# Attention values stored before their division, their sums read back from DRAM, and copies moved earlier in SyncE's list

## What is computed

```python
xn = layernorm(x)                                  # x: 8 batches x 1024 tokens x 256
q, k, v = xn @ Wq.T, xn @ Wk.T, xn @ Wv.T          # 16 heads of q, 8 of k and v, 16 wide
energy = q @ k.T + alibi                           # per batch and head, 1024 x 1024
attn = softmax(energy / 4)
att = (attn @ v) -> concat heads
out = x + att @ Wo.T + bo + quantised_linear(xn)   # int8 weights, one scale per token
```

## Time and profile before

| | |
|---|---|
| three timed runs | 1606.62, 1609.25, 1608.16 us, median 1608.16 |
| the profiled execution | 1606.43 us, its span 1604.5 us |
| busy in the span | PE 1507.3 (94%), DVE 1394.1 (87%), ACT 1183.8 (74%), POOL 1073.4 (67%) |
| DMA | 140.98 MB, 88 GB/s, 16 DMA engines about a third busy |
| granted TensorE clock | 0.978 of 2.4 GHz on the mean |

### The profile page before, as it was taken

The page is one execution under the profiler, slowest core; times in us unless marked ns, Lnnn a source line. Parts: engine busy times, 40 slices in busy tenths (PEclk is TensorE's granted clock), DMA queues, the critical chain, the costliest instruction groups (busy, mean ns, idle before and its releaser), DMA issues.

```text
span 1604.5 us, 42517 instructions
## 1 busy us (share of the span) xinstructions
PE 1507.3 (94%) x16284; PEld 584.2 (36%) x16284; DVE 1394.1 (87%) x1698; ACT 1183.8 (74%) x2331; POOL 1073.4 (67%) x1627
## 2 busy tenths in 40 slices
PE   5789989999899998999989999899998999899999
PEld 5323323333333333333333334333333333233333
DVE  6889989999799997999979999799987988899991
ACT  3467777777687775887757887677776777688885
POOL 6457877777688875787757787577785776433332
PEclk9899999999999999999999999999999999999999
DMA  6423233343324333333333333333333332212211
GB/s 169 130 62 84 71 99 79 89 98 84 105 72 106 96 79 98 93 93 101 84 84 95 103 90 90 89 94 97 94 86 85 95 85 69 80 44 70 70 42 61
DMA packets 197291, 140.98 MB, mean 88 GB/s; under 512 B 107040, under 2 KB 165728, under 8 KB 197088
## 3 DMA queue, kind: packets, MB, share of 16 engines
q1 hardware_dynamic: 197088, 138.27, 33.0%
HBM read 81.40 MB, written 35.63 MB: 73 GB/s over the span
## 4 chain that ended last, share of the span: by engine, by line
PE 53%; DVE 31%; issue 8%; SPq 4%; DMA 3%; POOL 0%; ACT 0%; POOLq 0%; ACTq 0%
DVE row_max L999 29%; PE ps_ring L1279 17%; PE ps_pv L1355 15%; PE ps_row L1296 11%; PE ps_ring L1395 4%; PE ps_ring L1415 3%; DMA q_again<-q 2%; PE ps_ring L1398 1%; DVE pv_turned L1039 1%; PE ps_row L1279 1%; PE ps_ring L1409 1%; SPq L497 1%; PE ps_row L1387 1%; SPq L464 0%; DMA base<-x 0%
## 5 line engine op out<-in xcount | busy, mean ns | idle before, releaser
L999 DVE TENSOR_REDUCE row_max<-ps_row 128x1 f32<-128x1024 f32 x1024 | 1199.2, 1213 | 153.8 <-PE ps_row L1298 138.5
L1171 ACT ACTIVATE probs<-ps_ring 128x512 f32<-128x512 f32 x2048 | 1083.7, 601 | 284.8 <-PE ps_ring L1279 282.3
L1279 PE MATMUL ps_ring<-q,k 122*32 122x512 bf16 x8192 | 639.2, 385 | 5.6 <-DMA q<-neg_max_t 4.7
L762 POOL TENSOR_TENSOR probs<-probs,near 128x256 f32<-128x256 f32 x512 | 374.2, 731 | 368.5 <-ACT probs L1171 362.8
L1355 PE MATMUL ps_pv<-probs,v_unit 128*32 128x512 f32 x4096 | 537.9, 601 | 0.0
L1279 PEld LDWEIGHTS ps_ring<-q,k 122*32 122x32 bf16 x8192 | 216.5, 95 | 511.7 <-ACT probs L1171 324.6
L1296 PE MATMUL ps_row<-k,q 64*128 64x512 bf16 x944 | 329.7, 390 | 68.1 <-DMA q_again<-q 43.2
L1298 PE MATMUL ps_row<-k_again,q_again 64*128 64x512 bf16 x944 | 329.6, 390 | 0.0
L1296 PEld LDWEIGHTS ps_row<-k,q 64*128 64x128 bf16 x944 | 83.9, 93 | 362.9 <-issue 197.8
L1355 PEld LDWEIGHTS ps_pv<-probs,v_unit 128*32 128x32 f32 x4096 | 125.2, 110 | 55.1 <-issue 9.1
L1298 PEld LDWEIGHTS ps_row<-k_again,q_again 64*128 64x128 bf16 x944 | 83.8, 93 | 0.0
(11 more groups left out here) (84 smaller groups left out, 1009.1 us busy)
## 6 DMA issues: line engine op xcount, KB each, us to landing
parts_dram<-parts SPq DMA_DIRECT2D x59, 288.0 KB, 3.3
q_again<-q SPq DMA_DIRECT2D x63, 256.0 KB, 3.4
token_b<-token_dram SPq DMA_DIRECT2D x53, 256.0 KB, 4.0
q<-parts_dram SPq DMA_DIRECT2D x128, 96.0 KB
k<-parts_dram SPq DMA_DIRECT2D x256, 32.0 KB
q<-parts_dram SPq DMA_DIRECT2D x128, 64.0 KB
att_dram<-att_unit SPq DMA_DIRECT2D x126, 64.0 KB
att_t<-att_dram SPq DMA_DIRECT2D x56, 128.0 KB, 2.9
```

The lines of the kernel that those rows point to most:

```text
L762: pool.tensor_tensor(here, here, near[:, u % KV_HEADS, :].rearrange("p (e n) -> p e n", e=GROUP), ALU.mult).then_inc(weighted, 1)
L999: dve.tensor_reduce(row_max[:, par, e, qb:qb + 1], ps_row[qb % 2][:, :], AX_X, ALU.max, negate=True).then_inc(row_max_found, 1)
L1171: act.activation(probs[:, c % PBUFS, e, h * HALF:(h + 1) * HALF], ring_bank(u, c, e, h), ACT.Exp, scale=SCALE).then_inc(ring_freed, 1)
L1279: mm = pe.matmul(to[at, :], weights[:, at], moving, start=start, stop=stop)
```

## The change

Values are no longer turned, divided and turned back. ScalarE copies `ps_pv` as it is (`keep_pv`, one operation of 128x512 in slot 1 of the next unit), SP stores that with one DMA, and, within the loads of the next set (after its k rows), reads the sums back as 128x16 (`load_sums`). VectorE takes their reciprocal in slot 6 (`find_rsum`), SP stores it (`store_rsum`). For each pair of tiles SP loads the raw values (`load_att_t`, two DMAs) and the reciprocals spread over the 16 rows of each head (`load_att_r`, two DMAs), and GpSimd multiplies them (`share`, one operation of 128x512) in slot 0 of the odd unit, behind `weigh_near` and `shift_turned`; TensorE's `outputs` waits for that product. The last batch is projected behind its units, before as now (`project_last`, L1387); its values are now divided by VectorE (`share_last`), all but the last unit's, which are still turned, divided and turned back.

In SP's list the copies of a late set move from the end of a unit's list to its beginning, `store_att` stands ahead of the next set, and at the start the first `place_max` stands ahead of the copies of set 2 and of `load_token`.

```diff
             def load_set(u, slot, between=None):
...
+                if between is not None:
+                    load_sums(between)
...
             def store_att(u):
-                wait(sp, att_unit_ready, u + 1)
-                for e in range(GROUP):
...
+                sp.wait_ge(pv_read, u + 1)
+                sp.dma_start(att_dram[u // KV_HEADS, u % KV_HEADS].rearrange("e h r n -> (e h r) n"),
+                             att_raw[:, u % 2, :]).then_inc(att_stored[u % 2], 16)
+            def load_sums(u):
+                sp.wait_ge(att_stored[u % 2], 16 * (u // 2 + 1))
+                wait(sp, rsum_ready, u - 1)
+                sp.dma_start(sums[:, u % 2, :],
...
+            def load_att_r(t):
+                b, at = t // BLOCKS, t % BLOCKS * P
+                wait_units(rsum_stored, (b + 1) * KV_HEADS)
...
             load_set(2, 2)
+            load_again(1, 1)
...
             store_token(PREP_AHEAD)
+            place_max(0, 0)
+            load_again(2, 2)
             load_token(PREP_AHEAD)
-            load_again(1, 1)
-            load_again(2, 2)
-            place_max(0, 0)
 
             def unit(u, f):
...
+                if u + 2 < UNITS and late_set(u + 2):
+                    load_again(u + 2, (u + 2) % SETS)
+                if f["prev"]:
+                    store_att(u - 1)
                 if f["row_set"] and not late_set(u + 3):
-                    next_set(u + 3)
-                if u % PAIR == 1:
-                    store_att(u - 1)
+                    next_set(u + 3, u - 1 if f["prev"] else None)
+                elif f["prev"]:
+                    load_sums(u - 1)
...
                     place_max(u + 1, (u + 1) % SETS)
-                if f["prev"] and u % PAIR == 0:
-                    store_att(u - 1)
-                for t in f["next_att"]:
-                    load_att_t(t, t % 2)
+                for t in f["next_att"][:1]:
+                    load_att_t(t)
+                if f["prev"] and not f["last"]:
+                    store_rsum(u - 1)
                 if f["row_set"]:
                     if late_set(u + 3):
                         next_set(u + 3)
                     else:
                         load_again(u + 3, (u + 3) % SETS)
-                if u + 2 < UNITS and late_set(u + 2):
-                    load_again(u + 2, (u + 2) % SETS)
+                for t in f["next_att"][:1]:
+                    load_att_r(t)
                 for t in finished(u):
                     store_out(t, t % 2)
...
+            def share(t):
+                pool.wait_ge(att_t_loaded, 16 * 2 * EC * (t // PAIR + 1))
+                pool.tensor_tensor(att_t[:, :, :], att_t[:, :, :], att_r[:, :, :],
+                                   ALU.mult).then_inc(att_t_ready, 1)
...
-                    if c == 3 and f["prev"] and u % PAIR == 0:
-                        norm(u - 1)
+                    if c == 0:
+                        for t in f["proj"][:1]:
+                            share(t)
...
+                        if i == 13 and f["prev"]:
+                            find_rsum(u - 1)
...
+            def keep_pv(u):
+                act.wait_ge(pv_done, BLOCKS * (u + 1))
+                wait(act, att_stored[u % 2], 16 * (u // 2))
+                act.activation(att_raw[:, u % 2, :], ps_pv[:, :], ACT.Copy).then_inc(pv_read, 1)
...
+                    if c == 1 and f["prev"]:
+                        keep_pv(u - 1)
...
-                        pe.wait_ge(att_t_loaded[t % 2], 16 * (t // 2 + 1))
+                        pe.wait_ge(att_t_ready, t // PAIR + 1)
```

More of the change, by code:

```diff
@@ L64 @@
 V_COLS = 32
+SUMS = GROUP * SEQ // P
 LN_EPS = 1e-5
@@ L450, in wait_parts, with load_set @@
                     wait(sp, parts_stored[t % 2], 16 * len(range(t, tiles, 2)))
-            def load_set(u, slot):
+            def load_set(u, slot, between=None):
                 g, tok = u % KV_HEADS, (u // KV_HEADS) * SEQ
@@ new lines, in wait_units, with heads_of, load_att_t @@
+            def wait_units(stored, units):
+                for i in range(2):
+                    sp.wait_ge(stored[i], 16 * len(range(i, units, 2)))
+            def heads_of(c):
+                return slice(c * (KV_HEADS // EC), (c + 1) * (KV_HEADS // EC))
+            def load_att_t(t):
+                b, half, at = t // BLOCKS, t % BLOCKS // (BLOCKS // 2), t % (BLOCKS // 2) * P
+                wait_units(att_stored, (b + 1) * KV_HEADS)
+                if t >= PAIR:
+                    wait_filled(sp, projected_unit(t - PAIR), "outputs", 1)
+                for c in range(EC):
+                    sp.dma_start(att_t[:, c, :],
+                                 att_dram[b, heads_of(c), :, half, 0:HEAD_DIM, at:at + PAIR * P].rearrange(
+                                     "g e d n -> (g e) d n")).then_inc(att_t_loaded, 16)
@@ L640, in next_set, with load_att_last @@
                     wait_filled(sp, u - SETS, BLOCKS - 1, GROUP - 1, 1)
-                load_set(u, u % SETS)
-            def load_att_last(c, rows, units):
-                sp.wait_ge(att_stored, 16 * GROUP * units)
-                sp.dma_start(att_last[0:rows, c, :],
-                             att_dram[c * P:c * P + rows, TOKENS - SEQ:TOKENS]).then_inc(
-                                 att_last_loaded[c], 16)
+                load_set(u, u % SETS, between)
+            def load_att_last(c, groups, units):
+                g = slice(c * (KV_HEADS // EC), c * (KV_HEADS // EC) + groups)
+                heads = groups * GROUP
+                wait_units(att_stored, units)
+                for half in range(2):
+                    sp.dma_start(att_last[0:heads * HEAD_DIM, c, 0, half * HALF:(half + 1) * HALF],
+                                 att_dram[BATCH - 1, g, :, half, 0:HEAD_DIM, :].rearrange(
+                                     "g e d n -> (g e) d n")).then_inc(att_last_loaded[c], 16)
+                wait_units(rsum_stored, units)
+                sp.dma_start(att_last[0:heads * HEAD_DIM, c, 1, :],
+                             rsum_dram[BATCH - 1, g, :, :].rearrange(
+                                 "g e n -> (g e) n").unsqueeze(1).broadcast_to(
+                                     [heads, HEAD_DIM, SEQ])).then_inc(att_last_loaded[c], 16)
             def store_out(t, par):
@@ L850, in unit @@
             def unit(u, f):
-                t = u + PREP_AHEAD
+                turned = u + PREP_AHEAD
                 for c in range(BLOCKS):
@@ L854, in unit @@
                     if c == 0 and f["turned"]:
-                        shift_turned(t)
+                        shift_turned(turned)
                     if c == 1:
@@ L1377, in ahead_row_block @@
                     project_last(0, P, slots)
-                if i % 2 == 0 and slots >= BLOCKS + 2:
-                    project_last(1, P - GROUP * HEAD_DIM, slots - BLOCKS - 2)
             def project_last(c, rows, i):
```

154 lines of the change are left out of this document (71 added, 83 removed).

## The result

The changed kernel takes 1672.73 us (median of four, 1668.82 to 1677.63), the kernel before 1607.83 in the same comparison: ratio 1.0405, 95% interval 1.037 to 1.044. It is 4% slower, where 1595 and a gain were forecast, and it lies outside the range of 1572 to 1624. The profiled execution is the slowest of the four, 1677.63 us with a span of 1675.9, so the traces differ by 71.4 us where the medians differ by 64.9. Parts are taken from the traces, verdicts from the medians. (An issue is SP's instruction that starts a transfer; the transfer has landed when what waits for it can go on.)

The account below looks back on a forecast made before the run. It took even units as bounded by a loop of TensorE, ScalarE and VectorE, odd units additionally by TensorE's slot 1. Terms summed to -12.3 us from 1606.4 profiled: 1594, or 1596 from the median; forecast 1595, range 1572 to 1624.

Parts of the forecast that it names:

- Late copies, -55.6: Units 7, 15, ... 55: TensorE's waits for late copies, and what follows them, all go; -55.6 us.
- What stands behind them, +9: SP's list before units 7, 15, ... 55: later maxima make TensorE wait 1.3 us, seven times; +9 us (2 to 16).
- The upper bound of 2.3 us a unit: Top of the predicted range, 0.3 to 2.3 us, for each of the seven waits for the maxima.
- The product on GpSimd, +46: Odd units, slot 1: TensorE waits 1.96 us for GpSimd's product in 22 units, plus 3 us elsewhere; +46 us.
- the loads should just land by then: Odd units: GpSimd's list decides the product's start; its loads, landing near 873, should not hold it.
- VectorE, -7: Even units: without VectorE's steps on the values, 0.22 us less, 31 times; -7 us (bounds -14 and 0).
- the rival that was to strike all of them: Maxima late in every even unit: one microsecond later, 24 more units wait 0.7 us; 1604 to 1620, chance 0.09.
- Unit 1, -3.5: Unit 1: TensorE's 1.91 us wait for VectorE goes, and half of 3.41 us at slow clock; -3.5 us.
- The start, -4.7: Kernel start: the first maxima go out about 60, ending TensorE's 4.74 us wait; -4.7 us (-2 if weight loads hold it).
- The end, +2.5: Last batch: three more projections behind the last pv_block, about 1.3 us, and share_last stopping TensorE about 1.2; +2.5 us.
- ScalarE, +1: ScalarE's copy of ps_pv, 128x512, fits its idle time; +1 us in all (0 to 3).
- The rival of the falling clock: Odd units: slow clock follows the new waits, 1.7 us each, 37 us if all 22 fall; 1604 to 1632, chance 0.22.

Follow-up runs that it names:

- e3: The kernel before with only the late set's copies moved, to the head of SP's list; 1573.6 us, ratio 0.9802.
- e4: The kernel before with only the late set's copies moved, behind the loads of the next set; 1555.36 us, ratio 0.9674.
- e5: The changed kernel with GpSimd's product written over the reciprocals and TensorE waiting for the loads alone, output left undivided; 1613.78 us, ratio 1.0036.
- e1: The changed kernel with the late set's copies behind the next set's loads, not at the head of SP's list; 1649.23 us, ratio 1.0244.
- e2: The changed kernel with GpSimd's product ahead of shift_turned, directly behind the slot's first weigh_near; 1662.29 us, ratio 1.0318.
- e6: The changed kernel with late copies behind the next set, product ahead of shift_turned, and reciprocal loads ahead of load_again; 1613.34 us, ratio 1.0036.
- e7: e1 with the sums loaded behind the whole next set and the reciprocal two steps later, in slot 7; 1669.74 us, ratio 1.0367.
- e8: e4 with the changed kernel's start order, first maxima ahead of set 2's copies and load_token; 1549.12 us, ratio 0.9644.

## Why the prediction was wrong, step by step

**Late copies, -55.6: right.** e3 and e4 show 51.7 and 54.8. In the changed kernel itself the seven units show only 30.8, because two other terms lie in the same units: the product in slot 1 of the six that project (8.8 by e5), and the half speed in their slot 0, 4.51 us in unit 31 where 2.6 is usual, some 12 over seven units.

**What stands behind them, +9: the step that failed first.** The seven units ahead became 36.3 longer, and with those 12 the term is about 49 where 9 was put. Five things in unit 30 were larger than estimated. The landing of the late set was put at 1.0 us; SP stood 2.9. The list began 0.5 later in the unit than before. Three loads that take 1.34 (in e1 and before) took 2.28, and the sums stood 0.7 for the store. From the last issue to TensorE it was 1.9 us (852.35 to 854.23), not the 1.2 taken from the start. That is 4.7 us on top of the 1.3 predicted, 6.0; TensorE's matmul waited 5.03, its weight load 5.74. The upper bound of 2.3 us a unit was no bound, and the prediction's own rows said so: in the earlier trace rows a transfer of the same list, the upper copy for unit 32, takes 3.8 us from issue to TensorE. That the copies' wait itself, and not only the number of issues, makes the maxima late is shown by e1 (16.7 less) and by e3 against e4 (16.6): in all four kernels the copies stand ahead of the maxima. What e1 has left above e4 in these units, another 16.6, belongs to the rest of the change (the store, the sums, 17.5 MB more traffic); no run tells these apart.

The Trainium skill ("DMA: Bandwidth & Descriptors", section "Latency and other measured facts") gives an access to HBM 0.2 us on the mean and 2 at high load, and lays most of a transfer's fixed time to it. In the trace the store of 256 KB lands after 2.0 us on the median, and after 3.5 to 5.0 in these seven units, where it follows two copies; in e1, where it follows the late set's loads instead, after 3.7 to 4.7. No run here tells a slower access from standing in the queue behind other transfers.

**The product on GpSimd, +46: right in kind, too small, and the second step that failed.** It cost 59.7 in the 17 odd units, some 9 in the seven units 7, 15, ... 55 (8.8 by e5), and 7.5 in units 53, 57, 59 and 61, where the prediction had put 0.2 each and the product stood for the loads: some 76. In the common unit the step was good: 1.96 us were predicted, 1.83 measured (the product took 1.26 to 1.40 us, the estimate was 1.10), and 2.2 on the unit. 17 times 2.2 is 37. What failed is "the loads should just land by then". In nine of the 17 they landed after GpSimd was free, and these waits are 9.8 us longer together than 1.83 each; in a tenth, unit 19, GpSimd itself came 0.8 later. The last 12 us are half-speed stretches behind six of the 17 waits. e2, e5 and e6 show the first two: with the product early the loads hold it, with the product off the path 44.9 goes, with both mended most common waits go.

The Trainium skill ("GPSIMD Engine Reference", section "Elementwise — side-by-side cycle accounting") has 4497 ns for an fp32 `tensor_tensor` addition with N = 2048. A quarter of that, an estimate from this page's figure, is 1.12 us for 512 columns; the runs show 1.26 to 1.40, so 0.14 to 0.28 more.

**VectorE, -7: right in its window, taken back in the next.** Slots 0 to 3 fell from 10.25 to 10.01 in unit 34, as the earlier trace rows promised; slots 4 to 7 rose to 10.13. e7, where the reciprocal stands two steps later, has 10.02, which points to the reciprocal's place in slot 6. The prediction had this as its bound of nothing. Beyond it, seven of the 23 common even units (2, 4, 20, 32, 40, 42, 50) end with late maxima, 0.5 to 1.2 us each, the rival that was to strike all of them. All 23 together are 468.01 us, before 466.17.

**Unit 1, -3.5:** 3.2, right, though its half for the clock may be luck: the half-speed stretch is gone from unit 1 in e3 and e8 too, where VectorE still has its four steps. **The start, -4.7:** 2.1; the maxima go out at 61.93 but four issues take 4.31 us behind the large weights, so the first quarter comes at 70.25, not 4.7 earlier; the prediction's other bound, -2, was the right one. **The end, +2.5:** 1.3. **ScalarE, +1:** not to be told apart. Added up by the traces (-52 to -55, +49, +76, +2 for VectorE, -3, -2, +1) the parts make +68 to +71; the spans differ by 71.4.

**The rival of the falling clock** (0.22, up to 1632) came true in part, in six of the 17 units, and behind the maxima, where the prediction had not looked for it. Nor did every such wait bring the slow clock, as the prediction had it from the rule that idle time brings it back: eleven of the 17 were followed by none. The third fault of the working lies here: the rivals were weighed as alternatives, each with its own time, though the late maxima, the late loads and the fall of the clock can all come at once, and did. What decides which wait is followed by half speed stays open, and the length alone does not: TensorE's wait of 3.12 us in unit 17 was followed by none, that of 1.83 us in unit 35 was. No run here isolates it.

## What to carry to other kernels

An issue moved ahead in an in-order list takes its own wait along: ask what it waits for, read from a loaded stretch of the same program how long such a transfer takes to land, and put it behind the transfers that others need first (e3 and e4 differ by 18 us for that alone). An operation put between a load and TensorE can add its whole length and the queue ahead of it on its engine, unless load and engine are both early, as here in unit 27 of e6; mending one of the two showed only a part (e2). And try the parts of a change alone: of this one the late copies, put behind the set, are worth 3.3%, and with the new start the kernel stands 3.6% below the one before.

## What the runs showed of the hardware that was not expected

- A single wait of TensorE of 1.83 us, with full work on both sides, is followed by 3.41 us at 0.50 of the 2.4 GHz in unit 35 and by none in unit 27 of the same execution. Of the waits in the same 17 units, six are followed by half speed in the changed kernel and eleven in e1.
- Two kernels with such waits scatter more from run to run than the kernel before, which lies between 1604.78 and 1610.73 in nineteen runs: on the same chip e6 lies between 1603.06 and 1623.80 in ten, e5 between 1606.30 and 1619.45 in ten. That the waits are the cause is not shown.
- A 128x512 product on GpSimd takes 1.26 to 1.40 us, and the four issues of `place_max` take 2.7 us in the middle of the program and 4.31 at the start of the changed kernel, issued right behind the loads of the weights (3.17 in the kernel before, which issues them later).
